# Adapter products with the tokens as stationary operand, beside the main products, in a two-layer LoRA kernel on one core

## The chip, the cores and the metric

The kernel runs on one core of one Trainium2 chip. The time is the device time of one execution in microseconds; lower is better. Matrix products run on TensorE (PE in the profile). In front of each matmul its stationary operand (up to 128 rows by 128 columns) is loaded into the array by a weight load, which the profile lists as an engine of its own, PEld. The moving operand (up to 512 columns) is then streamed through. VectorE (DVE) and ScalarE (ACT) do elementwise work, GpSimd (POOL) and SyncE (SP) mostly issue DMAs here.

## The reference

Two linear layers with a residual each, each with a low-rank adapter that is picked per batch entry:

```python
# x: (8, 256, 1024), one adapter index per batch entry and layer, rank 16
x = x + (x @ W.T + b) + 2 * (x @ A0[i0]) @ B0[i0]          # layer 0
x = x + (x @ W1.T + b1) + (x @ A1[i1].T) @ B1[i1].T        # layer 1
```

## The kernel before

The two layers are folded into one. A first part (up to about 130 us) multiplies the two matrices (I + W0) and (I + W1) into one 1024 by 1024 matrix D, and makes for each batch the low-rank remainder of both adapters: per batch entry 16 columns from layer 0 and 16 columns g that carry layer 1's adapter back through layer 0, with 98 rows (`STACK` = 6 x 16 + 2) on the other side, `rb`, that hold the ranks' second factors and the bias in split form. Every float32 operand is split into a high and a low part of type float32r (`hi`, `lo`), and a product is hi x hi + hi x lo + lo x hi.

The second part runs over the 8 batches `b` of 256 tokens. The main product (256 x 1024 by 1024 x 1024) is done as Strassen-Winograd: seven products `p1` to `p7` of half size. Each (`product`, L855 to L863) is 12 matmuls with 512 moving columns: four blocks k of the contraction, three passes each, on L860 (hi x hi), L861 (hi x lo), L862 (lo x hi). The tokens are stationary (128 token columns of `xa` or of a sum S1 to S4), the weights move. The quarters of the input are A11, A21, A12, A22, where the first digit is the half of the tokens `q`.

The adapters' first factors are multiplied by `h_product` (L869 to L881): there the factors `aa` are stationary and the tokens move, 16 matmuls with 256 moving columns on L880, into bank 6 or 7. DVE then splits the 32 rows of the sum (`stack_h`, L583 to L596) into `h_stack`, and four matmuls per batch on L867 (`ranks`) add the low-rank part and the bias into the four output quarters. The bias part that passes through layer 1's adapter is added to the bias rows in the first part: L847 multiplies `t_blk` by `b1_raw` in plain float32, beside L846.

Order and waiting are written by hand: each engine has its own list of instructions, with semaphores between them. Per batch from the second on PE does p1, h_product, p6, p2 and its rank, p5, p7, p4 and its rank, `fill_z` (a rank), p3 and its rank. SP issues in each batch, after the store of the batch before, the four loads of the next batch's quarters in the order A11, A21, A12, A22 (`load_x`, L209 to L217). DVE's list for a batch interleaves the low parts (`low_x`, L534), the sums S1 to S4 (L541 to L558), `factors` of the next batch (L573 to L577) and the output combinations (`make_u2`, `make_u4`, `make_u3`, `put_c21`, `put_c22`, `put_c12`, L606 to L635). ACT makes the high parts (`high_x`, L376), `keep_p1` and `put_c11`.

Of the kernel before, what the change touches and what calls it, by code (L numbers as in the profile page):

```python
# [23 lines left out]
def lora_pair(nc, xT, W0, W1T, A0, B0T, A1T, B1, b0, b1, idx0, idx1, out):  # L24
# [12 lines left out]
    AA_W = KT * 4 * RK + 4 * RK  # L37
# [6 lines left out]
    with ExitStack() as ctx:  # L44
# [11 lines left out]
        xa = sb("xa", [P, 2, 4, QW], F32R)  # L56
        a1 = sb("a1", [P, KT, 2 * BR], F32R)
        b0w = sb("b0w", [P, KT, 2 * BR + 2], F32R)
        aa = sb("aa", [P, 2, AA_W], F32R)
# [8 lines left out]
        h_sum = sb("h_sum", [2 * RK, T], F32)  # L68
        t_blk = sb("t_blk", [P, B], F32)
# [12 lines left out]
        h_tmp = scratch[0:32, 0:T]  # L82
# [23 lines left out]

        def x_op(j, part):
            if j <= A22:
                return xa[:, part, j, :]
            at = (3 * KH + j - S1) * HALF  # L110
            return w1[:, part, at:at + HALF]
# [17 lines left out]
        X, Z, Y, V, W = (banks[i] for i in (2, 3, 4, 5, 0))  # L129
# [42 lines left out]
        ones_set = sem("ones_set")  # L172
        pad_set = sem("pad_set")
        aa_hi = sem("aa_hi")
        aa_ready = sem("aa_ready")
        op_hi = [sem(f"op_hi{j}") for j in range(8)]
        op_lo = [sem(f"op_lo{j}") for j in range(8)]
        s_made = {j: sem(f"s_made{j}") for j in (S1, S2, S3, S4)}
        h_summed = sem("h_summed")
        h_moved = sem("h_moved")  # L180
        h_added = sem("h_added")
        h_hi = sem("h_hi")
        h_ready = sem("h_ready")
        p_done = [sem(f"p_done{n}") for n in range(8)]
        z_full = sem("z_full")
# [21 lines left out]
        def _(sp):  # L207
            def load_x(b):
                for j in (A11, A21, A12, A22):  # L209
                    if b >= 1:  # L210

                        sp.wait_ge(op_lo[j], b)
                        for s in {A11: (S2, S3), A21: (S1, S3), A12: (S4,), A22: (S1,)}[j]:
                            sp.wait_ge(s_made[s], b)
                        if j in (A21, A12):
                            sp.wait_ge(op_lo[S3 if j == A21 else S4], b)
                    sp.dma_start(xr[:, j, :], xT[b, :, j, :]).then_inc(x_landed[j], DMA)  # L217

            def load_rb(b):
                if b >= 2:  # L220
                    sp.wait_ge(p_done[3], b - 1)
                    sp.wait_ge(p_done[4], b - 1)
                    sp.wait_ge(p_done[2], b - 1)
                    sp.wait_ge(z_full, b - 1)
# [94 lines left out]
        def _(act):  # L319
# [43 lines left out]
            def high_x(j, b):  # L363
# [4 lines left out]
                if b >= 1:  # L368

                    if j == A21:  # L370
                        act.wait_ge(h_summed, b)
                    else:
                        act.wait_ge(p_done[LAST_USE[j]], b)
                    if j <= A22:
                        act.wait_ge(h_summed, b)
# [14 lines left out]
            def put_c11(b):  # L390
                act.wait_ge(p_done[2], b + 1)
# [3 lines left out]

            for k in range(KT):
# [17 lines left out]
            for j in (A11, A21, A12, A22):  # L414
                high_x(j, 0)

# [23 lines left out]
            high_t(T3)  # L440
            put_c11(0)
            for j in (A11, A21, A12, A22, S2, S1):
                high_x(j, 1)
            for b in range(1, B):
                if b == 1:
                    for j in (S4, S3):
                        high_x(j, 1)
                else:
                    high_x(S4, b)
                keep_p1(b)  # L450
                if b + 1 < B:
                    high_x(A11, b + 1)
                    high_x(A21, b + 1)
                    high_x(S2, b + 1)
                put_c11(b)
                if b + 1 < B:
                    high_x(A12, b + 1)
                    high_x(S1, b + 1)
                    high_x(S3, b + 1)
                    high_x(A22, b + 1)  # L460

        @block.vector
        def _(dve):
# [86 lines left out]
            def sum_s3(b):  # L550

                dve.wait_ge(op_lo[A21], b + 1)
# [12 lines left out]
            def factors(b):  # L565
                s = b % 2
                to = aa[:, s, 0:KT * 4 * RK].rearrange("p (k c) -> p k c", k=KT)
                g = g_all[:, :, b * RK:(b + 1) * RK]
                a0 = a0_raw[:, s, :].rearrange("p (k r) -> p k r", k=KT)
                dve.wait_ge(a0_landed[s], (b // 2 + 1) * DMA)  # L570
                if b >= 2:
                    dve.wait_ge(h_summed, b - 1)
                nc.vector.tensor_copy(to[:, :, 0:RK], a0).then_inc(aa_hi, 1)  # L573
                nc.vector.tensor_copy(to[:, :, RK:2 * RK], g).then_inc(aa_hi, 1)
                dve.wait_ge(aa_hi, b * 2 + 2)
                nc.vector.tensor_tensor(to[:, :, 3 * RK:4 * RK], g, to[:, :, RK:2 * RK], ALU.subtract)
                nc.vector.tensor_tensor(to[:, :, 2 * RK:3 * RK], a0, to[:, :, 0:RK], ALU.subtract).then_inc(aa_ready, 1)  # L577

            def stack_h(b):
                s = b % 2  # L580
                bank = banks[6 + s]
                dve.wait_ge(h_summed, b + 1)
                nc.vector.tensor_copy(h_tmp, bank[2 * RK:4 * RK, 0:T]).then_inc(h_moved, 1)  # L583
                dve.wait_ge(h_moved, b + 1)
                nc.vector.tensor_tensor(h_sum[:, :], bank[0:2 * RK, 0:T], h_tmp, ALU.add).then_inc(h_added, 1)
                dve.wait_ge(h_added, b + 1)
                if b >= 2:

                    dve.wait_ge(p_done[2], b - 1)
                    dve.wait_ge(p_done[3], b - 1)  # L590
                    dve.wait_ge(p_done[4], b - 1)
                    dve.wait_ge(z_full, b - 1)
                nc.vector.tensor_copy(h_stack[s][0:2 * RK, :], h_sum[:, :]).then_inc(h_hi, 1)
                nc.vector.tensor_copy(h_stack[s][2 * RK:4 * RK, :], h_sum[:, :]).then_inc(h_hi, 1)
# [413 lines left out]
```

## Time and profile before

| | |
|---|---|
| median of 3 runs | 313.38 us (311.9 to 313.47) |
| the profiled execution, device time | 312.38 us |
| its span, first to last instruction | 310.8 us |
| PE busy | 298.8 us, 96% of the span |
| DVE busy | 193.7 us, 62% |
| ACT busy | 89.7 us, 29% |

The span is the time between the first and the last instruction of that one execution; the device time holds 1.6 us more. Times of instructions below count from the span's start. A matmul's listed duration covers its way through the array, which overlaps the next matmul's; what a matmul costs in a row of matmuls is the distance from its start to the next one's start.

### The profile page before, as it was taken

Reading aid. Unit: us, or ns where it says so; the run is one execution under the profiler, and the core shown is the slowest. Engines: PE = TensorE matmul, PEld = TensorE weight load, DVE = VectorE, ACT = ScalarE, POOL = GpSimd, SP = SyncE. Lnnn points to the kernel's source line nnn. Section 1 sums busy time; section 2 is a strip of 40 time slices with the busy share of each in tenths; the row PEclk is TensorE's granted clock in tenths of the full one; section 3 lists DMA queues with packets and bytes.
Section 4 is the critical chain, followed back from the end, with each engine's and each line's share of the span. In section 5 each row is a group of like instructions: output and inputs, shape, how many; then the busy total and the mean of one; then the engine's idle time right before and its main releaser. Section 6 shows DMA issues by size and latency. Waiting matters only on the chain.

```text
span 310.8 us, 3985 instructions
## 1 busy us (share of the span) xinstructions
PE 298.8 (96%) x1420; PEld 247.6 (80%) x1420; DVE 193.7 (62%) x325; ACT 89.7 (29%) x142; POOL 18.5 (6%) x43
## 2 busy tenths in 40 slices
PE   0999999999999999998999999999999999999995
PEld 0888898888887488886888888888888888888884
DVE  4777624994749362188896776487486485585312
ACT  4555424112123302293224123232232322232000
POOL 2443140000000010000000000000000000000000
PEclk9999999999999999999999999999999999999999
DMA  7996140000000155504054360440641621602002
GB/s 268 382 347 226 48 159 12 0 0 2 0 0 3 17 178 209 166 0 135 0 194 138 115 184 34 152 147 34 187 141 38 211 78 70 219 35 85 18 34 101
DMA packets 14456, 33.94 MB, mean 109 GB/s; under 512 B 2117, under 2 KB 2117, under 8 KB 14438
## 3 DMA queue, kind: packets, MB, share of 16 engines
q1 hardware_dynamic: 13414, 31.60, 30.1%
q0 software_dynamic: 1024, 2.10, 2.1%
q8 instruction: 11, 0.18, 0.2%
q14 instruction: 7, 0.06, 0.1%
HBM read 22.09 MB, written 11.60 MB: 108 GB/s over the span
## 4 chain that ended last, share of the span: by engine, by line
PE 92%; DVE 4%; ACT 2%; DMA 1%; issue 0%; SPq 0%
PE bank L766 29%; PE bank L861 16%; PE bank L860 16%; PE bank L862 16%; PE bank L880 4%; PE bank L778 3%; PE bank L867 3%; DMA stage<-W1T 1%; PE bank L835 1%; PE bank L837 1%; PE bank L836 1%; PE bank L780 1%; DVE w L562 1%; PE bank L808 1%; PE bank L846 1%; PE bank L847 1%
## 5 line engine op out<-in xcount | busy, mean ns | idle before, releaser
L766 PE MATMUL bank<-w,w_hi 128*128 128x512 f32 x256 | 80.7, 397 | 7.0 <-ACT w L325 7.0
L766 PEld LDWEIGHTS bank<-w,w_hi 128*128 128x128 f32 x256 | 48.7, 192 | 17.9 <-ACT w L325 7.0
L766 PE MATMUL bank<-w,w_lo 128*128 128x512 f32 x128 | 50.1, 391 | 0.0
L376 ACT CAST xa<-xr 128x512 fp32r<-128x512 f32 x32 | 19.6, 621 | 33.9 <-PE bank L867 15.0
L766 PEld LDWEIGHTS bank<-w,w_lo 128*128 128x128 f32 x128 | 24.2, 189 | 5.1
L861 PE MATMUL bank<-w_lo,w 128*128 128x512 f32 x64 | 25.1, 392 | 0.0
L862 PE MATMUL bank<-w_hi,w 128*128 128x512 f32 x64 | 25.0, 391 | 0.0
L860 PE MATMUL bank<-w_hi,w 128*128 128x512 f32 x64 | 25.0, 391 | 0.0
L861 PE MATMUL bank<-w 128*128 128x512 f32 x64 | 25.0, 391 | 0.0
L860 PE MATMUL bank<-w 128*128 128x512 f32 x64 | 25.0, 391 | 0.0
L860 PE MATMUL bank<-w_hi,xa 128*128 128x512 f32 x64 | 25.0, 390 | 0.0
L861 PE MATMUL bank<-w_lo,xa 128*128 128x512 f32 x64 | 24.9, 390 | 0.0
L862 PE MATMUL bank<-w 128*128 128x512 f32 x64 | 24.9, 389 | 0.0
L862 PE MATMUL bank<-w_hi,xa 128*128 128x512 f32 x64 | 24.9, 389 | 0.0
L534 DVE TENSOR_TENSOR xa<-xr,xa 128x512 fp32r<-128x512 f32 x32 | 21.1, 685 | 1.4 <-ACT xa L376 1.4
L529 DVE SCALAR_TENSOR_TENSOR rows<-w,b_raw,rows 128x1024 f32<-128x1024 f32 x16 | 20.5, 1283 | 0.4
L376 ACT CAST w<-rows 128x512 fp32r<-128x512 f32 x16 | 9.8, 621 | 37.7 <-DVE rows L548 25.9
L534 DVE TENSOR_TENSOR w<-rows,w 128x512 fp32r<-128x512 f32 x16 | 11.0, 687 | 11.9 <-ACT w L376 11.9
L376 ACT CAST w<-xr 128x512 fp32r<-128x512 f32 x16 | 9.8, 621 | 29.5 <-PE bank L867 15.8
L880 PEld LDWEIGHTS bank<-xa,aa 128*128 128x128 f32 x128 | 16.2, 189 | 0.6
L880 PE MATMUL bank<-xa,aa 128*128 128x256 f32 x128 | 16.4, 281 | 0.0
L778 PE MATMUL bank<-a,w_hi 128*128 128x256 f32 x64 | 15.5, 327 | 0.0
(119 smaller groups left out, 487.0 us busy)
## 6 DMA issues: line engine op xcount, KB each, us to landing
xr<-xT SPq DMA_DIRECT2D x32, 256.0 KB, 4.4
out<-stage SPq DMA_DIRECT2D x28, 256.0 KB, 2.1
stage<-W SPq DMA_DIRECT2D x8, 512.0 KB, 4.9
stage<-W1T SPq DMA_DIRECT2D x8, 512.0 KB, 6.0
a<-rb_rows SPq DMA_DIRECT2D x8, 392.0 KB
rb_rows<-a SPq DMA_DIRECT2D x3, 512.0 KB
rb_rows<-b0w SPq DMA_DIRECT2D x3, 512.0 KB
out<-rows SPq DMA_DIRECT2D x4, 256.0 KB, 2.2
```

Of the source, the lines that this page charges most:

```text
L376: nc.scalar.copy(x_op(j, 0), raw(j)).then_inc(op_hi[j], 1)
L529: nc.vector.scalar_tensor_tensor(out=bias_sum, in0=part[:, k, :], scalar=b0_raw[:, k:k + 1], in1=bias_sum, op0=ALU.mult, op1=ALU.add).then ...
L534: nc.vector.tensor_tensor(x_op(j, 1), raw(j), x_op(j, 0), ALU.subtract).then_inc(op_lo[j], 1)
L562: nc.vector.tensor_tensor(t_whole(t, 1), t_raw[t][:, :, :].rearrange("p k n -> p (k n)"), t_whole(t, 0), ALU.subtract).then_inc(t_lo, 1)
L766: return mm(d_bank(m, h)[:, :], left[:, m, k * P:(k + 1) * P], right[:, k, h * HALF:(h + 1) * HALF], start=start, stop=stop)
L778: last = mm(bank[:, 0:2 * BR], w0_hi[:, m, cols], a1[:, k, :], start=(k == 0), stop=(k == KT - 1))
L780: mm(bank[:, 0:BR], w0_lo[:, m, cols], a1[:, k, 0:BR], start=False, stop=False)
L860: mm(bank[:, :], hi, t_op(t, 0, k), start=(start and k == 0), stop=False, skip_group_check=not start)
L861: mm(bank[:, :], hi, t_op(t, 1, k), start=False, stop=False, skip_group_check=not start)
L862: last = mm(bank[:, :], lo, t_op(t, 0, k), start=False, stop=(k == KH - 1), skip_group_check=not start)
L867: return mm(bank[:, :], h_stack[b % 2][0:STACK, q * P:(q + 1) * P], rb[b % 2][:, h * HALF:(h + 1) * HALF], start=False, stop=True, skip_gr ...
L880: last = mm(banks[6 + s][:, 0:T], aa[:, s, k * 4 * RK:k * 4 * RK + P], xa[:, part, 2 * kh:2 * kh + 2, tok], start=(k == 0 and part == 0), ...
```

## The change

The first factors' product changes sides. For each 128-token column block that `p1`, `p2`, `p4` and `p5` load anyway, two more matmuls stand between the three of the product: the token block's high part by 64 columns of `aa` (`h_high`: 32 factor columns' high parts and 32 low parts), and its low part by the 32 high columns (`h_low`). The result has tokens on its rows: bank 6 for the first half of the tokens (`q` 0, closed in p2), bank 7 for the second (`q` 1, from S1 in p5 and A22 in p4, for which `factors` makes a third set of factor columns, the difference of the two halves). Quarter A21 is then needed in no operand, and its high and low parts go. `split_h` on DVE splits each half (128 rows by 32 columns, five operations), `turn_h` transposes it by a matmul against an identity in float32r (98 columns stationary, 128 moving), `stack_h` on ACT copies it into `h_stack`. The ranks' matmuls are taken out of p2, p3 and p4 and moved later.

The bias term through layer 1's adapter, L847's two float32 matmuls, goes; in its place `t_sum` is split, turned by one matmul with an identity (a row ahead of the `r` products), copied by ACT to `t_rows`, and added to the sum by a matmul of two stationary rows and 16 moving columns, once per half (`ones_row`, `t_rows`).

On PE, where a batch begins. Before: the end of the batch before (L867), p1, the adapter product (L880), then p6:

```order
L867 MATMUL bank<-a,b0w 128x512
L860 MATMUL bank<-w_hi,xa 128x512 [waits op_lo0,made_c11]
L861 MATMUL bank<-w_lo,xa 128x512
L862 MATMUL bank<-w_hi,xa 128x512
...
L880 MATMUL bank<-xa,aa 128x256 [waits op_lo2,op_lo3,op_lo1,h_added,op_lo0,aa_ready]
L880 MATMUL bank<-xa,aa 128x256 x15
L860 MATMUL bank<-w 128x512 [waits op_lo5,kept_u3]
```

The adapter product stands there as one block of 16.

After, the same place: L896, L901 and L906 are the three passes of a product, L913 is `h_high`, L916 `h_low`, L909 the bias rows:

```order
L927 MATMUL bank<-a,b0w 128x512 [waits h_stacked,kept_u4]
L896 MATMUL bank<-w_hi,xa 128x512 [waits h_read0,op_lo0,made_c11,aa_ready]
L913 MATMUL bank<-aa,xa 128x64
L901 MATMUL bank<-w_lo,xa 128x512
L916 MATMUL bank<-aa,xa 128x32
L906 MATMUL bank<-w_hi,xa 128x512
L909 MATMUL bank<-t_rows,ones_row 128x16
L896 MATMUL bank<-w_hi,xa 128x512
L913 MATMUL bank<-aa,xa 128x64
```

Sixteen matmuls in one block have become 34 small ones per batch, each between two matmuls of 512 columns.

On PE behind the last auxiliary product of the first part (L806), after the change; the row with 2x128 is new, and the next row stood directly behind L806's before:

```order
L857 MATMUL bank<-ident_r,t_parts 2x128 [waits aux_done,consts_set,t_split]
L865 MATMUL bank<-rows,s_t 128x512 [waits b1_landed,st_step,t4_made]
```

The small turn of `t_parts` waits for `aux_done` 8, the end of DVE's `g_add(7)`, which L865 does not wait for.

On DVE in batch 0, after the change; L637 is `make_u2`, L644 `make_u4`, L666 `put_c12`, L569 and L576 the sums S1 and S2 of batch 1, L562 the low parts of A11, S2, A12, and L617 to L627 `split_h(0, 1)`:

```order
L637 TENSOR_TENSOR stage<-bank,rows 128x512 [waits t_lo,kept_p1,p_done6]
L644 TENSOR_TENSOR stage<-bank,stage 128x512 [waits kept_u2,p_done5]
L666 TENSOR_TENSOR stage<-bank,stage 128x512 [waits kept_u4,full_c12]
L569 TENSOR_TENSOR rows<-xr 128x512 [waits op_lo4,x_landed3,x_landed1]
L576 TENSOR_TENSOR rows<-rows,xr 128x512 [waits s_made4,op_lo5,x_landed0]
L562 TENSOR_TENSOR xa<-xr,xa 128x512 [waits op_hi0]
L562 TENSOR_TENSOR w<-rows,w 128x512 [waits op_hi5]
L562 TENSOR_TENSOR xa<-xr,xa 128x512 [waits op_hi2]
L617 COPY h_small<-bank 128x32 [waits h_summed1]
L619 TENSOR_TENSOR h_sum<-bank,h_small 128x32 [waits h_moved1]
L624 CAST h_parts<-h_sum 128x32 [waits h_read1]
```

The second split of batch 0 stands behind eight operations of 512 columns. In the later batches the sums S1 and S2 of the next batch have moved ahead of `make_u2` and of the first split.

The diff, cut to its core:

```diff
             def factors(b):
...
+                nc.vector.tensor_tensor(f_raw[:, KT:both, :], f_raw[:, KH:KT, :], f_raw[:, 0:KH, :], ALU.subtract
+                                        ).then_inc(f_step, 1)
...
+            def split_h(b, q):
+
+                dve.wait_ge(h_summed[q], b + 1)
+                nc.vector.tensor_copy(h_small[:, q, :], H[q][:, FW:2 * FW]).then_inc(h_moved[q], 1)
+                dve.wait_ge(h_moved[q], b + 1)
+                nc.vector.tensor_tensor(h_sum[:, q, :], H[q][:, 0:FW], h_small[:, q, :], ALU.add
+                                        ).then_inc(h_read[q], 1)
...
+            pe.wait_ge(t_split, 2)
+            pe.wait_ge(consts_set, 3)
+            pe.wait_ge(aux_done, 8)
+            mm(banks[7][0:2, 0:P], t_parts[:, :], ident_r[:, :], start=True, stop=True).then_inc(t_turned, 1)
...
-                mm(bank[0:B, :], ones_b[:, :], bias_sum[:, cols], start=True, stop=False)
-                mm(bank[0:B, :], t_blk[:, :], b1_raw[:, cols], start=False, stop=True).then_inc(c_summed, 1)
+                mm(bank[0:B, :], ones_b[:, :], bias_sum[:, cols], start=True, stop=True).then_inc(c_summed, 1)
...
                     mm(bank[:, :], hi, t_op(t, 0, k), start=(start and k == 0), stop=False, skip_group_check=skip)
+                    if closes:
+                        h_low(b, h, k, lo)
+                    elif h is not None:
+                        h_high(b, h, k, hi, opens, False)
+                    mm(bank[:, :], hi, t_op(t, 1, k), start=False, stop=False, skip_group_check=skip)
+                    if closes:
+                        h_high(b, h, k, hi, False, True).then_inc(h_summed[h[0]], 1)
+                    elif h is not None:
+                        h_low(b, h, k, lo)
+                    last = mm(bank[:, :], lo, t_op(t, 0, k), start=False, stop=(k == KH - 1), skip_group_check=skip)
+                    if opens:
+
+                        mm(H[h[0]][:, RK:FW], ones_row[:, :], t_rows[:, b * RK:(b + 1) * RK], start=False, stop=False)
...
+            def h_high(b, h, k, hi, start, stop):
+                return mm(H[h[0]][:, 0:2 * FW], hi, aa[:, b % 2, h[1] * KH + k, :], start=start, stop=stop)
+
+            def h_low(b, h, k, lo):
+                return mm(H[h[0]][:, 0:FW], lo, aa[:, b % 2, h[1] * KH + k, 0:FW], start=False, stop=False)
+
+            def turn_h(b, q):
+                pe.wait_ge(h_split[q], b + 1)
+                if 2 * b + q > 0:
+                    pe.wait_ge(h_stacked, 2 * b + q)
+                mm(H_TURNED[0:STACK, q * P:(q + 1) * P], h_parts[:, q, :], ident_r[:, :], start=True, stop=True
+                   ).then_inc(h_turned, 1)
...
-            def h_product(b):
...
-                for k in range(KT):
...
             for b in range(1, B):
                 p1(b)
-                h_product(b)
                 p6(b)
                 p2(b)
                 p5(b)
+                turn_h(b, 0)
+                p4(b)
+                rank11(b)
                 p7(b)
-                p4(b)
-                fill_z(b)
-                p3(b)
+                turn_h(b, 1)
+                p3(b, first)
+                rank21(b)
+                rank22(b)
+                p3(b, second)
+                rank12(b)
```

## Rows read from the trace of the kernel before

**Rows 1.** The page: busy shares, and the chain that ended last, by engine.

```profile
PE 298.8 (96%) x1420; PEld 247.6 (80%) x1420; DVE 193.7 (62%) x325; ACT 89.7 (29%) x142; POOL 18.5 (6%) x43
...
PE 92%; DVE 4%; ACT 2%; DMA 1%; issue 0%; SPq 0%
```

**Rows 2.** TensorE's clock in 40 slices, in tenths of full speed, from the page.

```profile
PEclk9999999999999999999999999999999999999999
```

**Rows 3.** Timeline of PE in one batch: start us, us, line, operands, count.

```profile
175.54 0.40 PE L860 MATMUL bank<-w_hi,xa 128*128 128x512 f32 x1
...
178.28 2.05 PE L880 MATMUL bank<-xa,aa 128*128 128x256 f32 x16
180.17 0.40 PE L860 MATMUL bank<-w 128*128 128x512 f32 x1
...
197.51 0.40 PE L860 MATMUL bank<-w_hi,xa 128*128 128x512 f32 x1
```

**Rows 4.** Timeline of PE, an auxiliary product of the first part between 512-column matmuls.

```profile
75.07 0.39 PE L766 MATMUL bank<-w,w_lo 128*128 128x512 f32 x1
75.30 0.28 PE L778 MATMUL bank<-a,w_hi 128*128 128x256 f32 x1
75.41 0.22 PE L780 MATMUL bank<-a,w_lo 128*128 128x128 f32 x1
...
77.14 0.63 PE L766 MATMUL bank<-w,w_hi 128*128 128x512 f32 x2
```

**Rows 5.** Timeline of the weight loads (PEld) at the same place.

```profile
75.08 0.19 PEld L778 LDWEIGHTS bank<-a,w_hi 128*128 128x128 f32 x1
75.30 0.19 PEld L780 LDWEIGHTS bank<-a,w_lo 128*128 128x128 f32 x1
75.42 0.19 PEld L778 LDWEIGHTS bank<-a,w_hi 128*128 128x128 f32 x1
```

**Rows 6.** Timeline of PE and PEld inside a product.

```profile
158.17 0.40 PE L860 MATMUL bank<-w 128*128 128x512 f32 x1
158.17 0.19 PEld L861 LDWEIGHTS bank<-w 128*128 128x128 f32 x1
```

**Rows 7.** Timeline of PE at the bias rows.

```profile
105.55 1.02 PE L847 MATMUL bank<-rows,t_blk 128*8 128x512 f32 x2
106.41 1.02 PE L846 MATMUL bank<-rows,ones_b 128*8 128x512 f32 x2
```

**Rows 8.** Timelines of PE and DVE behind the last auxiliary product.

```profile
91.73 1.02 PE L832 MATMUL bank<-rows,s_t 128*128 128x512 f32 x2
...
92.35 0.28 DVE L492 TENSOR_TENSOR g_all<-bank,scratch 128x128 f32<-128x128 f32 x1
```

**Rows 9.** Timeline of PE in batch 0, and where batch 1 begins.

```profile
130.11 0.39 PE L860 MATMUL bank<-w_hi,xa 128*128 128x512 f32 x1
...
141.54 0.50 PE L867 MATMUL bank<-a,b0w 98*128 98x512 f32 x1 [1.19 <-DVE b0w L596]
...
153.56 0.39 PE L860 MATMUL bank<-w_hi,xa 128*128 128x512 f32 x1
```

**Rows 10.** Timeline of DVE in batch 0.

```profile
136.58 2.29 DVE L562 TENSOR_TENSOR w<-stage,w 128x2048 fp32r<-128x2048 f32 x1
...
142.13 4.49 DVE L562 TENSOR_TENSOR w<-stage,w 128x2048 fp32r<-128x2048 f32 x2
```

**Rows 11.** Groups of DVE by line: busy us, mean ns of one, idle before.

```profile
L583 DVE COPY scratch<-bank 32x256 f32<-32x256 f32 x8 | 3.3, 416 | 19.4 <-PE bank L880 19.3
...
L606 DVE TENSOR_TENSOR stage<-bank,rows 128x512 f32<-128x512 f32 x4 | 2.7, 686 | 1.2 <-PE bank L862 1.2
```

**Rows 12.** Timeline of SP at the next batch's loads.

```profile
177.03 1.83 SPq L217 DMA_DIRECT2D xr<-xT  x4
```

**Rows 13.** The loads' time from issue to landing, from the line's own view.

```profile
DMA to landing us min/median/max: 3.1/4.4/5.8
```

**Rows 14.** Timeline of DVE at the end.

```profile
307.58 0.69 DVE L635 TENSOR_TENSOR stage<-bank,stage 128x512 f32<-128x512 f32 x1 [1.74 <-PE bank L867]
```

More of the change, by code:

```diff
@@ L105, in t_whole @@
             return w1[:, part, at:at + KH * HALF]
+        XA = (A11, A12, A22)
         def x_op(j, part):
-            if j <= A22:
-                return xa[:, part, j, :]
+            if j in XA:
+                return xa[:, part, XA.index(j), :]
             at = (3 * KH + j - S1) * HALF
@@ L390, in put_c11 @@
             def put_c11(b):
[L391 removed]
+                act.wait_ge(full["c11"], b + 1)
                 if b >= 2:
@@ L413, in _ @@
             aux_copy(8)
-            for j in (A11, A21, A12, A22):
+            for j in XA:
                 high_x(j, 0)
+            act.wait_ge(t_turned, 1)
+            nc.scalar.copy(t_rows[:, :], banks[7][0:2, 0:P]).then_inc(t_rows_made, 1)
             for h in range(NH):
@@ L676, in _ @@
             bias_add(7)
-            for j in (A11, A21, A12, A22):
+            for j in XA:
                 low_x(j, 0)
@@ L708, in _ @@
             low_t(0, T2)
[L710 to L713 removed]
+            split_h(0, 0)
             low_x(S3, 0)
@@ L718, in _ @@
             make_u4(0)
-            for j in (A11, A21, A12, A22):
-                low_x(j, 1)
+            put_c12(0)
             sum_s1(1)
             sum_s2(1)
-            make_u3(0)
-            low_x(S2, 1)
-            put_c21(0)
-            put_c22(0)
-            put_c12(0)
+            for j in (A11, S2, A12):
+                low_x(j, 1)
+            split_h(0, 1)
             sum_s3(1)
@@ L756, in _ @@
                 put_c22(b)
-                if b + 1 < B:
-                    low_x(A22, b + 1)
                 put_c12(b)
@@ L909, in p3, with rank12 @@
                     pe.wait_ge(made["c12"], b)
-                product(b, S4, B22, W, True)
-                ranks(b, 0, 1, W).then_inc(p_done[3], 1)
+                last = product(b, S4, B22, W, True, ks)
+                if ks[-1] == KH - 1:
+                    last.then_inc(p_done[3], 1)
+            def rank12(b):
+                ranks(b, 0, 1, W).then_inc(full["c12"], 1)
             def p4(b):
@@ L917, in p4, with rank21 @@
                     pe.wait_ge(made["c21"], b)
-                product(b, A22, T4, V, True)
-                ranks(b, 1, 0, V).then_inc(p_done[4], 1)
+                product(b, A22, T4, V, True, h=(1, 2)).then_inc(p_done[4], 1)
+            def rank21(b):
+                ranks(b, 1, 0, V).then_inc(full["c21"], 1)
             def p5(b):
@@ L942, in p7 @@
                 pe.wait_ge(kept["u2"], b + 1)
-                product(b, S3, T3, Y, False).then_inc(p_done[7], 1)
-            pe.wait_ge(pad_set, 2)
+                last = product(b, S3, T3, Y, False, ks)
+                if ks[-1] == KH - 1:
+                    last.then_inc(p_done[7], 1)
+            first, second = range(KH // 2), range(KH // 2, KH)
             p1(0)
-            h_product(0)
             p5(0)
@@ L950, in _ @@
             p3(0)
+            turn_h(0, 0)
             p6(0)
+            rank11(0)
+            rank12(0)
             p4(0)
-            fill_z(0)
-            p7(0)
+            p7(0, first)
+            turn_h(0, 1)
+            p7(0, second)
+            rank21(0)
+            rank22(0)
             for b in range(1, B):
                 p1(b)
-                h_product(b)
                 p6(b)
```

238 lines of the change are left out of this document (122 added, 116 removed).

## The prediction

> **What bounds the kernel now.** I read the busy shares and the chain that ended last first: PE is busy 96% of the span and carries 92% of that chain [rows 1], and its granted clock stays at the full level, 2.4 GHz, in all slices [rows 2]. So the time is the sum of what PE issues, plus the few places where it waits. Next the timeline of one batch: p1 begins at 175.54 and the next batch's p1 at 197.51, 21.97 us, in which PE never stops. p1 takes 178.28 - 175.54 = 2.74 us, 0.228 us for each of 12 matmuls with 512 columns, and the adapter product 180.17 - 178.28 = 1.89 us, 0.118 us for each of 16 with 256 columns [rows 3]. DVE at 62% has room. The question is what a matmul with 64 or 32 moving columns costs between two of 512.
>
> **What a small matmul costs.** The trace has none that small, but it has 256 and 128 columns in turn. A stretch of 16, half of them 256 and half 128 wide, begins at 75.30 and the next 512-column matmul at 77.14: 1.84 us, 0.115 us each [rows 4]. Their columns are 3072, at 2.4 GHz 1.28 us, so columns do not set that pace. The weight loads do: those of consecutive matmuls start 0.12 us apart (75.30, 75.42) [rows 5], one per matmul, also for L860 and L861, which have the same tokens stationary (PE and PEld both count 1420) [rows 1, 6]. And a load does not run further ahead than one matmul: L780's load starts at 75.30, the moment L778 begins, although the load before it started at 75.08 [rows 4, 5]; in a product L861's load starts with L860's matmul at 158.17 [rows 6]. Under a 512-column matmul (0.228 us) a load of 0.116 us is hidden. Under a matmul of 64 or 32 columns it is not: the next product matmul's load can start only when the small one starts, and takes its 0.116 us. So each small matmul adds 0.116 us, whatever its width. The bounds: from below its columns alone, with the 0.013 us by which 0.228 us exceeds 512 columns at 2.4 GHz rounded up to 0.015: 0.042 us for 64 columns, 0.028 for 32, 0.022 for 16, 0.068 for 128. From above 0.12 us, the spacing of the loads as printed, unless the small form is treated in another way (a rival). I take 0.116, since the 128-column rows are nearest and are already bound by the load.
>
> The Trainium skill states another floor: by its page "TensorE: Matmul & The Clock Gate", section "Wait — 56ns, not 53.3ns?", matmuls start as little as 25 ns apart however small they are, and N columns cost N/2.4 + 2.5 ns. By that a batch's 36 new matmuls cost 1.0 us, less than the 1.89 us that go, and the kernel gets some 7 us faster; the rows with 128 columns (0.115 us where this rule has 0.056) speak against it, since each matmul here has its own load.
>
> **The change part by part.**
> 1. *The adapter product.* Removed per batch: 1.89 us [rows 3]. Added per batch: 16 pairs of h_high and h_low, 2 bias rows, 2 turns, 36 matmuls at 0.116 = 4.18 us. Net +2.29 us per batch, 8 batches: **+18.3 us**, all on PE's path. The low bound by columns is 16 x 0.042 + 16 x 0.028 + 2 x 0.022 + 2 x 0.068 = 1.30 us per batch, net -0.59, in all -4.7 us.
> 2. *The bias rows.* L847's two float32 matmuls cost 106.41 - 105.55 = 0.86 us each (the row's x2 is one instruction in two records) [rows 7]: **-1.7 us**. The added turn of t_parts costs 0.12 us.
> 3. *The wait in front of that turn.* It waits for `aux_done` 8. PE reaches this place at 91.73; the g_add that ends this count runs from 92.35 to 92.63 on DVE, behind low_bottom(6) [rows 8]. Everything behind it in PE's list, the r products first, waits too: 0.9 us, **+0.9 us**. The matmuls of r never waited for it before. Bounds 0.8 and 1.1.
> 4. *Batch 0, the wait that goes.* The rank in p2 waited for `stack_h`: PE idle 1.19 us, and the batch took 153.56 - 130.11 = 23.45 us, 1.48 more than a steady one [rows 9]. In the new order the first split has p3 to hide in: **-1.5 us**.
> 5. *Batch 0, the wait that comes.* With T0 the start of p1: p1 and p5 take 2.74 + 9 x 0.116 = 3.8 each, p2 2.74 + 0.93 = 3.7, so the first sum is whole at T0 + 11.2. DVE is free by then (its 2048-column L562 ended at 138.87, T0 + 8.8) [rows 10]. A split is five operations: 256 columns take 0.416 us and 512 take 0.686 [rows 11], so 0.00105 us a column over 0.15 us fixed, 0.18 for 32, and 0.03 between dependent ones: 1.05 us, T0 + 12.2. Then low_x(S3) 0.6, two L562 4.5 [rows 10], T0 + 17.3; then the eight operations of 512 columns at 0.69 to 0.72, of which two wait for ACT's part, T0 + 23.0; then the split, T0 + 24.1. PE: p1, p5, p2 11.2, p3 2.74, turn 0.12, p6 2.74, two ranks 0.47, p4 3.67, half of p7 1.37: it reaches `turn_h(0, 1)` at T0 + 22.3. It waits 1.8 us: **+1.8 us**; queued behind it are the second half of p7, the two ranks and batch 1. Bounds 0.8 (operations back to back at 0.60) and 3 (a load that lands late holds sum_s1).
> 6. *Later batches.* DVE now does the next batch's S1 and S2 ahead of the first split; S1 needs A22. SP issues the four loads 1.5 us to 3.3 us behind p1's start, the last one's issue beginning near +2.9 [rows 3, 12], and landing takes 4.4 to 5.8 us [rows 13]: A22 is there by +7.3 to +8.7. Then S1, S2, A11, make_u2, S2's low part, 5 x 0.65 = 3.2, and the split 1.05: done by +11.6 to +13.0. PE reaches `turn_h(b, 0)` at 3.8 + 2.74 + 3.7 + 3.7 = +13.9. It fits, with 0.9 to 2.3 us to spare. `turn_h(b, 1)` has p7 and a rank (3.0 us) for a split of 1.05. So these cost nothing; if the cover goes they cost the lateness of A22 itself. In batch 1 the loads start late, since DVE left batch 0 late: **+0.4 us**, bounds 0 and 1.5.
> 7. *DVE and ACT.* A21's low and high parts go (0.69 and 0.62 us a batch); the splits' ten small operations come to 2.1 us against 2.0 before, the copies of `stack_h` to ACT. Both stay off the path. The end keeps its order: the last rank, `put_c12` [rows 14], its store, and the two stores before it are done sooner or at the same time: 0.
>
> **The sum.** 18.3 - 1.7 + 0.1 + 0.9 - 1.5 + 1.8 + 0.4 = +18.3 us. Against the profiled execution's 312.38 us: 330.7 us. That execution lies 1.0 us under the median of the runs shown, so the median may be up to 1 us more; I take 331.
>
> **The rivals.**
> - *The loads are hidden (faster).* If the load of the small matmul and the one behind it both fit under the 512-column matmul in front, or a load of tokens that are already in place is left out, a small matmul costs its columns. The point from which it decides is a price under 0.05 us per small matmul. For it: three matmuls in five of a block share their stationary tokens. Against it: the loads' start with the matmul before, and L860 and L861, each with a load of its own [rows 4 to 6]. It gives 312.4 - 4.7 + 0.0 (terms 2 to 6) = 308 us. Chance 0.08.
> - *Half hidden.* A price of 0.08 us per small matmul, halfway between the bounds, gives 36 x 0.08 = 2.9 us per batch, +1.0 net: 320.3 us. Chance 0.05. The skill's same page, section "Back-to-back issue gap", has about 81 ns for pairs of load and matmul at 128 columns, which is this case; the rows show 115.
> - *A turn waits in every batch.* If A22 lands 1 us or more behind +8.7, or a split takes 2 us instead of 1, `turn_h(b, 0)` holds PE 1 to 2 us in seven batches: 338 to 345 us. For it: DVE's list is in strict order and S1 now stands first. Chance 0.06.
> - *The small float32r form is slow.* If 64 or fewer columns went as plain float32 does, in four passes of columns and loads as on L846, a small matmul would cost near 0.4 us and the kernel over 400 us. The 128-column rows show nothing of that. Chance 0.01.
> - That the change does not do what it says: the new order shows each matmul where the diff puts it.
>
> **How the numbers follow.** The forecast's own case has 0.80: 331 us. Its own range, with 0.113 to 0.12 us per small matmul (288 of them, -0.9 to +1.2), the waits (-1.8 to +3) and 1 us between executions, is 327 to 336. I take 325 to 336, a little to the half-hidden case; the rest is outside. A measurement of this kernel can tell about 0.5% from no change. Faster by over 0.5% is the first rival, 0.08; slower by over 0.5% is all the others, 0.91; within 0.5% 0.01.
>
> **What would show it.** In the changed kernel's trace: L913, L916 and L909 rows each followed 0.11 to 0.12 us later by the next matmul, with one load each; PE and PEld both at about 1577 (1420 - 128 - 4 + 288 + 1); a batch of 24.2 to 24.3 us; PE idle about 0.9 us in front of L857 and 1 to 3 us in front of the second L922 of batch 0, both put down to DVE; no idle time at L922 later. A batch under 22 us would show the first rival, idle time on each first L922 of a batch the third. Wrong is the forecast if loads run two matmuls ahead.

## The result and the profile after

The changed kernel takes 337.48 us in the median of 5 runs (335.97 to 341.43) against 312.74 for the kernel before: ratio 1.078, 95% interval 1.076 to 1.080. It is slower, as forecast, by 24.7 us instead of 18.3, and 1.5 us above the range. The profiled execution took 341.43 us (span 339.7); it has a stretch in which PE ran at half its clock, which not every execution has, so the sizes of steady batches below are read outside that stretch.

The page's lines on PE and on its clock, the ones of [rows 1, 2]:

```profile
PE 324.6 (96%) x1577; PEld 268.3 (79%) x1577; DVE 191.3 (56%) x364; ACT 88.3 (26%) x152; POOL 18.6 (5%) x43
...
PEclk9999999999999999999978999999999999999999
```

PE is still the bound, with 157 more matmuls and as many more loads; two slices of the clock are below 9.

The timeline of PE and PEld where a steady batch begins (start us, us, line, operands), to be held against [rows 3 to 6]:

```profile
187.24 0.39 PE L896 MATMUL bank<-w_hi,xa 128*128 128x512 f32 x1
...
187.47 0.19 PE L913 MATMUL bank<-aa,xa 128*128 128x64 f32 x1
187.47 0.19 PEld L901 LDWEIGHTS bank<-w_lo,xa 128*128 128x128 f32 x1
187.50 0.47 PE L901 MATMUL bank<-w_lo,xa 128*128 128x512 f32 x1
...
187.81 0.18 PE L916 MATMUL bank<-aa,xa 128*128 128x32 f32 x1
187.81 0.19 PEld L906 LDWEIGHTS bank<-w_hi,xa 128*128 128x128 f32 x1
187.84 0.48 PE L906 MATMUL bank<-w_hi,xa 128*128 128x512 f32 x1
188.24 0.18 PEld L909 LDWEIGHTS bank<-t_rows,ones_row 2*128 2x128 f32 x1 [0.24 <-issue]
188.24 0.27 PE L909 MATMUL bank<-t_rows,ones_row 2*128 2x16 f32 x1
188.44 0.19 PEld L896 LDWEIGHTS bank<-w_hi,xa 128*128 128x128 f32 x1
188.44 0.50 PE L896 MATMUL bank<-w_hi,xa 128*128 128x512 f32 x1
...
189.12 0.19 PEld L906 LDWEIGHTS bank<-w_hi,xa 128*128 128x128 f32 x1
189.23 0.19 PEld L896 LDWEIGHTS bank<-w_hi,xa 128*128 128x128 f32 x1
189.46 0.39 PE L896 MATMUL bank<-w_hi,xa 128*128 128x512 f32 x1
...
190.37 0.39 PE L896 MATMUL bank<-w_hi,xa 128*128 128x512 f32 x1
```

How to read it: the load of the matmul behind a small one starts when the small one starts (L901's at 187.47), as the rows before had it. L901's listed start of 187.50 lies 0.03 us behind that, and its duration is 0.47 instead of 0.39; I read the 0.08 us more as its wait for its load. A block without bias rows takes 190.37 - 189.46 = 0.91 us: three times 0.227 and two small ones at 0.115. The first block takes 189.46 - 187.24 = 2.22 with the second, 1.31 alone: L909 costs 0.40 us. In the block without bias rows the load behind L906's starts 0.11 us behind it (189.12, 189.23). L909's load starts 0.43 us behind L906's (187.81, 188.24), with nothing loading for the last 0.24 us, and the next 128-row load starts another 0.20 us later (188.44).

The batches, counted from 0: first the first turns of batches 4 and 5; then batch 0 with its second turn, and batch 1 with its first turn, each with what held it.

```profile
251.43 0.22 PE L922 MATMUL bank<-ident_r,h_parts 128*98 128x128 f32 x1
...
276.27 0.22 PE L922 MATMUL bank<-ident_r,h_parts 128*98 128x128 f32 x1
```

```profile
130.82 0.39 PE L896 MATMUL bank<-w_hi,xa 128*128 128x512 f32 x1
...
154.90 0.30 PE L922 MATMUL bank<-ident_r,h_parts 128*98 128x128 f32 x1 [1.04 <-DVE h_parts L627]
...
156.95 0.40 PE L896 MATMUL bank<-w_hi,xa 128*128 128x512 f32 x1
...
173.87 0.43 PE L922 MATMUL bank<-ident_r,h_parts 128*98 128x128 f32 x1 [2.20 <-DVE h_parts L627]
```

A steady batch takes 24.84 us (21.97 in [rows 3]). Batch 0 takes 156.95 - 130.82 = 26.13 with 1.04 us idle. Batch 1 takes 187.24 - 156.95 = 30.29, 5.45 more than a steady one: 2.20 listed as idle, and most of the other 3.25 from the clock (in a_pad32 below, whose clock stayed full, batch 1 has 2.11 us idle and takes 183.66 - 156.42 = 27.24 us, 2.40 more than a steady one). SP and DVE in batch 1 show where the 2.20 come from:

```profile
158.77 2.77 SPq L243 DMA_DIRECT2D out<-stage  x3
161.65 1.85 SPq L233 DMA_DIRECT2D xr<-xT  x4
...
169.73 0.69 DVE L569 TENSOR_TENSOR rows<-xr 128x512 f32<-128x512 f32 x1 [7.31 <-DMA xr<-xT]
```

The four loads start 4.7 us behind p1 instead of 1.5 [rows 3, 12], since the stores of batch 0 stand ahead of them in SP's list; the last is issued by 163.5 and S1 begins at 169.73, 6 us later (the longest landing of L233's loads in this trace is 6.5 us). S1 keeps DVE still for 7.3 us, while the split waits behind it. The clock in stretches (us, busy us and counts of PE, PEld, DVE, ACT, POOL, clock, DMA):

```profile
165.00:170.00 5.00, 5.00 (x29) 4.15 (x27) 0.27 (x1) 0.62 (x1) 0.00 (x0) 1.00 0.77 222
170.00:175.00 5.00, 2.80 (x14) 2.22 (x13) 4.80 (x13) 1.80 (x4) 0.00 (x0) 0.84 0.01 2
175.00:180.00 5.00, 5.00 (x16) 4.13 (x16) 1.82 (x4) 0.12 (x1) 0.00 (x0) 0.50 0.00 0
180.00:187.24 7.24, 7.24 (x33) 5.95 (x33) 4.25 (x10) 1.89 (x4) 0.00 (x0) 0.98 0.12 44
```

The granted clock falls to half (1.2 GHz) in this stretch, in which PE had stood still from 171.67 to 173.87, and is full (2.4 GHz) again soon after 180; in 175 to 180 PE gets 16 matmuls done, where it had done 29 in 165 to 170.

The wait in front of the turn of `t_parts`, from the waits by engine (us in total, times, longest):

```profile
PE bank L857 <- DVE g_all L520: 0.9, 1, 0.9
```

### The profile page after: what moved, and what is told of

The parts are those of the page before. It is cut to its first block, busy times and chain, and to the rows that moved or that the text cites. A ratio compares the mean times of both kernels' runs of the same rounds, so it can differ in the third digit from the quotient of the medians.

```text
span 339.7 us, 4386 instructions
## 1 busy us (share of the span) xinstructions
PE 324.6 (96%) x1577; PEld 268.3 (79%) x1577; DVE 191.3 (56%) x364; ACT 88.3 (26%) x152; POOL 18.6 (5%) x43
## 4 chain that ended last, share of the span: by engine, by line
PE 48%; DMA 2%; DVE 2%; SPq 1%; issue 0%; DVEq 0%
PE bank L906 15%; PE bank L901 15%; PE bank L896 13%; PE bank L927 2%; DMA xr<-xT 2%; PE bank L913 1%; PE bank L909 1%; SPq L243 1%; PE bank L916 0%; PE bank L922 0%; SPq L233 0%; DVE rows L569 0%; DVE stage L661 0%; DVE stage L656 0%; DVE stage L666 0%
## 5 line engine op out<-in xcount | busy, mean ns | idle before, releaser
L906 PE MATMUL bank<-w_hi,xa 128*128 128x512 f32 x64 | 30.5, 476 | 0.0
L901 PE MATMUL bank<-w_lo,xa 128*128 128x512 f32 x64 | 30.5, 476 | 0.0
L794 PEld LDWEIGHTS bank<-w,w_lo 128*128 128x128 f32 x128 | 24.6, 192 | 5.3
L906 PE MATMUL bank<-w_hi,w 128*128 128x512 f32 x64 | 27.9, 436 | 0.0
L901 PE MATMUL bank<-w_lo,w 128*128 128x512 f32 x64 | 27.8, 435 | 0.0
L896 PE MATMUL bank<-w_hi,w 128*128 128x512 f32 x64 | 26.3, 410 | 0.0
L896 PE MATMUL bank<-w_hi,xa 128*128 128x512 f32 x64 | 26.0, 406 | 0.0
L569 DVE TENSOR_TENSOR rows<-xr 128x512 f32<-128x512 f32 x8 | 5.5, 690 | 34.9 <-DMA xr<-xT 34.9
L896 PE MATMUL bank<-w 128*128 128x512 f32 x64 | 25.1, 392 | 0.0
L906 PE MATMUL bank<-w 128*128 128x512 f32 x64 | 25.0, 391 | 0.0
L901 PE MATMUL bank<-w 128*128 128x512 f32 x64 | 25.0, 391 | 0.0
L913 PEld LDWEIGHTS bank<-aa,xa 128*128 128x128 f32 x96 | 18.7, 195 | 2.9
L916 PEld LDWEIGHTS bank<-aa,xa 128*128 128x128 f32 x96 | 18.9, 197 | 0.7
L562 DVE TENSOR_TENSOR xa<-xr,xa 128x512 fp32r<-128x512 f32 x24 | 16.3, 686 | 4.9 <-ACT xa L385 4.9
L913 PE MATMUL bank<-aa,xa 128*128 128x64 f32 x96 | 18.7, 194 | 0.0
L916 PE MATMUL bank<-aa,xa 128*128 128x32 f32 x96 | 17.3, 180 | 0.0
L415 ACT CAST b0w<-bank 98x128 fp32r<-98x128 f32 x16 | 4.3, 266 | 46.5 <-PE bank L922 46.5
```

Of the source, the lines that this page charges most:

```text
L415: nc.scalar.copy(h_stack[b % 2][0:STACK, q * P:(q + 1) * P], H_TURNED[0:STACK, q * P:(q + 1) * P]).then_inc(h_stacked, 1)
L562: nc.vector.tensor_tensor(x_op(j, 1), raw(j), x_op(j, 0), ALU.subtract).then_inc(op_lo[j], 1)
L569: nc.vector.tensor_tensor(s_raw[S1], xr[:, A21, :], xr[:, A22, :], ALU.add).then_inc(s_made[S1], 1)
L794: return mm(d_bank(m, h)[:, :], left[:, m, k * P:(k + 1) * P], right[:, k, h * HALF:(h + 1) * HALF], start=start, stop=stop)
L896: mm(bank[:, :], hi, t_op(t, 0, k), start=(start and k == 0), stop=False, skip_group_check=skip)
L901: mm(bank[:, :], hi, t_op(t, 1, k), start=False, stop=False, skip_group_check=skip)
```

## The experiments

My theory after the two traces: (a) each small matmul costs one load, 0.115 us, whatever its width; (b) the 16 bias-row matmuls cost 0.40 us each, because an operand with two rows is not loaded under the running matmul ahead of it; (c) the waits of batches 0 and 1 come from the order of DVE's list, and the clock follows the second. Rivals: the price is that of mixing widths or of columns, L909 is dear for its 16 columns, and the waits would only move.

**Leaving out the bias rows.** The kernel leaves out the bias term through layer 1's adapter.

```diff
-                    if opens:
-
-                        mm(H[h[0]][:, RK:FW], ones_row[:, :], t_rows[:, b * RK:(b + 1) * RK], start=False, stop=False)
```

> The changed kernel without the 16 bias-row matmuls L909 (two stationary rows, 16 moving columns, two per batch); the bias term through layer 1's adapter is left out of the result. In the changed kernel's trace such a matmul costs 1.31 - 0.91 = 0.40 us where the forecast had 0.116. My theory (L909 is the mis-sized term): 16 x 0.40 = 6.4 us less than the changed kernel, 331 us, and a steady batch of 24.84 - 0.8 = 24.04 us. Rival (L909 costs 0.116 like the other small ones, and the missing time lies elsewhere): 1.9 us less, a batch of 24.6 us.

Measured 331.86 us, ratio 1.060 (1.056 to 1.064), 5.6 us less than the changed kernel. The first turns of two batches:

```profile
244.88 0.22 PE L919 MATMUL bank<-ident_r,h_parts 128*98 128x128 f32 x1
...
269.02 0.22 PE L919 MATMUL bank<-ident_r,h_parts 128*98 128x128 f32 x1
```

A batch takes 24.14 us, 0.70 less: 0.35 us per L909, near the 0.40 read from the rows and far from 0.116. The term was mis-sized as the theory says. This run too has a stretch at half clock, behind 1.55 us idle in batch 1.

**128 rows instead of two.** The 126 added rows of t_rows are set to zero once.

```diff
-        t_rows = sb("t_rows", [2, P], F32R)
-        ones_row = sb("ones_row", [2, P], F32R)
+        t_rows = sb("t_rows", [128, P], F32R)
+        ones_row = sb("ones_row", [128, P], F32R)
...
+            nc.vector.memset(t_rows[:, :].bitcast(F32), 0.0).then_inc(consts_set, 1)
...
```

> The changed kernel with ones_row and t_rows as 128 rows, of which 126 of t_rows are zero, so that L909 has 128 stationary rows instead of two and computes the same. Theory: the short stationary operand (two rows) is what costs, so L909 falls to 0.115 us, a steady batch to 24.27 us and the time by 16 x 0.285 = 4.6 us, to 333 us. Rival: the 16 moving columns or the narrow output cost, or the switch to other tiles; then nothing changes (24.84 us a batch, 337.5 us).

Measured 335.66 us (331.89 to 337.03), ratio 1.069 (1.062 to 1.075). The same place in its timeline, and its first turns:

```profile
184.93 0.39 PE L897 MATMUL bank<-w_hi,xa 128*128 128x512 f32 x1
...
185.51 0.19 PEld L907 LDWEIGHTS bank<-w_hi,xa 128*128 128x128 f32 x1
...
185.62 0.19 PEld L910 LDWEIGHTS bank<-t_rows,ones_row 128*128 128x128 f32 x1
185.85 0.17 PE L910 MATMUL bank<-t_rows,ones_row 128*128 128x16 f32 x1
...
186.87 0.39 PE L897 MATMUL bank<-w_hi,xa 128*128 128x512 f32 x1
...
247.48 0.22 PE L923 MATMUL bank<-ident_r,h_parts 128*98 128x128 f32 x1
...
271.82 0.22 PE L923 MATMUL bank<-ident_r,h_parts 128*98 128x128 f32 x1
```

Two blocks take 186.87 - 184.93 = 1.94, less 0.91: 1.03 for the first, so L910 with the same 16 columns costs 0.12 us, and its load now starts 0.11 us behind L907's (185.51, 185.62) instead of 0.43. A batch takes 24.34 us (24.27 expected). The median gained only 1.8 us of the 4 that 8 batches give. The clock is a likely reason: its profiled run too has a stretch at half clock behind the wait of batch 1 (1.92 us idle there). Its fastest run, 331.89 us, is 4.1 us under the fastest of the changed kernel.

**32 rows instead of two**, the same edit with 32.

> As a_pad128, with 32 rows instead of 128. It tells whether the short operand costs for having less than the full 128 rows, or only when it is very short. Theory A (a load of another number of rows cannot start under the running matmul): L909 stays at 0.40 us, a steady batch 24.84 us, 337.5 us. Theory B (only fewer than 32 rows cost): 0.115 us, a batch of 24.27 us, 332 to 335.7 us like a_pad128.

Measured 337.19 us, ratio 1.080 (1.075 to 1.085). Its L910, from the view of the line (duration ns min/median/max, first and last start), and its first turns:

```profile
L910 PEld LDWEIGHTS bank<-t_rows,ones_row x16: 181/181/181, 131.3 to 319.3; 32*128 32x128 f32 x16
...
247.85 0.22 PE L923 MATMUL bank<-ident_r,h_parts 128*98 128x128 f32 x1
...
272.69 0.22 PE L923 MATMUL bank<-ident_r,h_parts 128*98 128x128 f32 x1
```

24.84 us a batch: 32 rows cost what two cost. The load itself is no longer than others (0.18 us listed, 0.19 for 128 rows); what differs is when it starts: here too nothing loads for 0.24 us in front of L910, while in a_pad128 no idle time stands there. By the Trainium skill, page "TensorE: Matmul & The Clock Gate", section "LDWEIGHTS (loading the stationary operand)", a load of 32 by 128 takes as long as one of 128 by 128; the listed durations agree with that, and the price of the matmul, three times as high, does not follow from it. The ranks' operand with 98 rows does not pay it (0.23 to 0.24 us behind a product, L927 in the timelines as L867 before). Somewhere between 32 and 98 rows lies the border; where was not tried.

**Wide small matmuls.** What they sum is then not the adapters' product.

```diff
-                return mm(H[h[0]][:, 0:2 * FW], hi, aa[:, b % 2, h[1] * KH + k, :], start=start, stop=stop)
+                return mm(H[h[0]][:, 0:8 * FW], hi, aa[:, b % 2, h[1] * KH:(h[1] + 1) * KH, :], start=start, stop=stop)
```

and h_low in the same way.

> The changed kernel with 256 moving columns in every h_high and h_low instead of 64 and 32; what they sum is then not the adapters' product. Theory (the load sets the price): 256 columns take 0.118 us in the kernel before, so at most 256 x 0.003 = 0.8 us more than the changed kernel, 338 us. Rival (the price is columns plus something fixed): 0.080 us more for each h_high and 0.093 for each h_low, 128 of each, +22 us, 360 us.

Measured 339.36 us, ratio 1.086 (1.083 to 1.089). One block in its timeline:

```profile
185.25 0.39 PE L896 MATMUL bank<-w_hi,xa 128*128 128x512 f32 x1
185.48 0.28 PE L913 MATMUL bank<-aa,xa 128*128 128x256 f32 x1
185.60 0.39 PE L901 MATMUL bank<-w_lo,xa 128*128 128x512 f32 x1
...
186.18 0.40 PE L896 MATMUL bank<-w_hi,xa 128*128 128x512 f32 x1
```

0.93 us a block against 0.91: four and eight times the columns cost 0.01 us each. A batch takes 25.21 us by two of its turns (248.09 and 273.30), 0.37 more; over 8 batches 3.0 us: more than the 0.8 expected, and nowhere near the 22 of a price by columns. The median grew by 1.9 us only; PE idles 0.97 and 1.49 us in batches 0 and 1 here, 0.8 less in all than in the changed kernel. So a narrower moving operand saves almost nothing below 256 columns.

**No h_low.** The 128 matmuls of the tokens' low part are left out.

```diff
-                    if closes:
-                        h_low(b, h, k, lo)
-                    elif h is not None:
+                    if h is not None and not closes:
                         h_high(b, h, k, hi, opens, False)
...
-                    elif h is not None:
-                        h_low(b, h, k, lo)
```

> The changed kernel without the 128 h_low matmuls (the tokens' low part times the factors is left out). Theory (one load each, 0.115 us): 128 x 0.115 = 14.7 us less, 322.8 us, a steady batch of 23.0 us; the stall of batch 1 may shrink or grow by a microsecond. Rival (a small matmul costs its columns, 0.028 us, and the rest is a cost of mixing that h_high alone brings): 3.6 us less, 334 us.

Measured 325.28 us, ratio 1.041 (1.035 to 1.046). A batch takes 23.00 us by its first turns (287.41 and 310.41), 1.84 less, 0.115 for each h_low, as expected. The time lies 2.5 us above the expected one. The waits grew, batch 0's from 1.04 to 1.52 us and batch 1's from 2.20 to 3.12:

```profile
170.76 0.30 PE L918 MATMUL bank<-ident_r,h_parts 128*98 128x128 f32 x1 [3.12 <-DVE h_parts L627]
```

A faster PE reaches the turn earlier, while the load hardly moves (S1 begins 12.2 us behind batch 1's p1, 12.8 before): a part of what PE saves there is given back as idle time. Behind the 3.12 us the granted clock fell again (0.66 in 170 to 175), which costs this execution 1.7 us more in batch 1 (24.69 us between the first turns of batches 1 and 2, against 23.00).

**The order of DVE's list in batches 0 and 1.**

```diff
-            for j in (A11, S2, A12):
-                low_x(j, 1)
-            split_h(0, 1)
+            low_x(A11, 1)
+            split_h(0, 1)
+            low_x(S2, 1)
+            low_x(A12, 1)
...
                     factors(b + 1)
+                if b == 1:
+                    make_u2(b)
+                    split_h(b, 0)
+                if b + 1 < B:
                     sum_s1(b + 1)
...
```

> The changed kernel with DVE's list reordered in batches 0 and 1 alone: the second split of batch 0 stands directly behind A11's low part, and in batch 1 make_u2 and the first split stand ahead of the sums S1 and S2 that wait for a load. Theory (the order of DVE's list makes the two waits of PE, 1.04 us and 2.2 us, and the half-clock stretch behind the second one follows from it): no idle time at either L922, PE's clock full in all slices, 3.2 us less without and up to 3.3 us more with the clock, 331 to 334 us. Rival (the wait moves: S1, now later, holds p6 or the first split of batch 2, and DVE stays behind): PE idles as long one batch later, 336 to 338 us.

Measured 334.06 us (333.66 to 334.82), ratio 1.067 (1.066 to 1.069), with the full clock in all slices of its page. DVE in batch 1:

```profile
166.15 0.19 DVE L617 COPY h_small<-bank 128x32 f32<-128x32 f32 x1 [2.67 <-PE bank L920]
...
167.22 0.69 DVE L569 TENSOR_TENSOR rows<-xr 128x512 f32<-128x512 f32 x1 [0.22 <-DMA xr<-xT]
```

The split is done before A22 lands, S1 waits 0.22 us, and PE is idle at no L922. 3.4 us are gone by the medians, at the upper end of the time expected (331 to 334); 3.2 are the two listed waits, and batches 0 and 1 take 24.85 and 24.88 us.

**The same edit in batch 1 alone.**

> a_order's edit in batch 1 alone; the second split of batch 0 stands where the change has it. Theory (the two waits are separate, batch 1's comes from S1's wait for the load of A22): the 1.04 us idle in batch 0 stays, none in batch 1, full clock: a_order plus 1.0 us, 335.1 us. Rival (batch 1's wait is the lateness that batch 0 hands on): idle time shows up in batch 1 again, at another instruction, 336 to 337.5 us.

Measured 335.42 us, ratio 1.074 (1.072 to 1.075). PE idles once, 1.04 us in front of batch 0's second turn, as in the changed kernel, and not in batch 1; the clock line of its page has a 9 in all slices. So the two waits are separate, and the fall of the clock goes with the second.

**The turn of t_parts behind the r products.**

```diff
-            pe.wait_ge(aux_done, 8)
-            mm(banks[7][0:2, 0:P], t_parts[:, :], ident_r[:, :], start=True, stop=True).then_inc(t_turned, 1)
-
             pe.wait_ge(t4_made, 2)
...
+            pe.wait_ge(aux_done, 8)
+            mm(banks[7][0:2, 0:P], t_parts[:, :], ident_r[:, :], start=True, stop=True).then_inc(t_turned, 1)
             pe.wait_ge(d_lo[B11], 3)
```

ACT's copy of its result moves behind the copies of r and b1 in the same way.

> The changed kernel with the small turn L857 and its wait for aux_done moved behind the r products, and ACT's copy of it behind the copies of r and b1. Theory: the wait of 0.9 us in front of it vanishes, since g_add has long ended there, and nothing else waits: 0.9 us less, 336.6 us. Rival (what stands behind is bound by DVE and ACT anyway, or the copy in ACT's list now delays the bias rows): no change.

Measured 335.9 us, ratio 1.074 (1.071 to 1.076). The median is 1.6 us under the changed kernel's, the fastest runs of both 0.7 us apart (335.29, 335.97). No wait in front of this matmul is left in the list of waits. The times cannot weigh the 0.9 us by itself: this execution also idles 1.32 us in batch 1 instead of 2.20, with the clock full, and p1 of batch 0 starts at 129.15 here, but anywhere from 129.38 to 130.90 in six executions that have the same first part as the changed kernel (its own among them). The 0.9 us is consistent, not measured.

**All three repairs.**

> The changed kernel with all three repairs: 128 stationary rows for the bias rows, the DVE order of a_order, the late turn. It computes the same. Theory: 4.6 + 3.2 + 0.9 us less and no half-clock stretch, 337.5 - 8.7 = 328.8 down to 326 us, a steady batch of 24.27 us; it stays slower than the kernel before by the weight loads, 8 x 2.29 = 18.3 us less the 1.7 + 1.5 us saved. Rival (something else of the new order costs): over 331 us.

Measured 328.42 us, ratio 1.051 (1.049 to 1.054). First turns of two batches:

```profile
264.04 0.22 PE L930 MATMUL bank<-ident_r,h_parts 128*98 128x128 f32 x1
...
288.35 0.22 PE L930 MATMUL bank<-ident_r,h_parts 128*98 128x128 f32 x1
```

24.31 us a batch. Against the kernel before (312.89 us beside it): 8 x (24.31 - 21.97) = 18.7, less 1.7 + 1.5 for the bias rows and batch 0's old wait, plus 0.1 for the turn, is +15.6; measured +15.5. What is left is the price of the small matmuls.

**The kernel before, with batch 0's rank behind p3.**

```diff
                 product(b, A12, B21, X, False)
+                if b > 0:
+                    rank11(b)
+
+            def rank11(b):
                 pe.wait_ge(h_ready, b + 1)
...
                 product(b, S4, B22, W, True)
+                if b == 0:
+                    rank11(b)
```

> The kernel before with one edit: in batch 0 the rank of p2 is issued behind p3's product instead of ahead of it, so that p3 hides stack_h. Theory (the 1.19 us of idle time there were all that held PE, as term 4 of the prediction has it): 1.2 to 1.5 us less, 311.4 us. Rival (DVE's list is the bound up to p4 and p7 of batch 0, and the wait moves there): no change.

Measured 311.39 us, ratio 0.9949 (0.9933 to 0.9965). PE over batch 0 in its windows view:

```profile
130.00:160.00 30.00, 30.00 (x149) 25.36 (x148) 26.44 (x39) 14.88 (x20) 0.00 (x0) 1.00 0.29 94
```

30 us busy of 30: the wait is gone and did not move.

**And with the bias term as a column that DVE adds.**

```diff
-                mm(bank[0:B, :], t_blk[:, :], b1_raw[:, cols], start=False, stop=True).then_inc(c_summed, 1)
...
+            mm(banks[7][0:2 * RK, 0:B], pick[:, :], t_blk[:, :], start=True, stop=True).then_inc(t_picked, 1)
...
-                nc.vector.tensor_tensor(h_sum[:, :], bank[0:2 * RK, 0:T], h_tmp, ALU.add).then_inc(h_added, 1)
+                nc.vector.scalar_tensor_tensor(out=h_sum[:, :], in0=bank[0:2 * RK, 0:T], scalar=t_cols[:, b:b + 1],
+                                               in1=h_tmp, op0=ALU.add, op1=ALU.add).then_inc(h_added, 1)
...
```

`pick` is a constant that DVE makes, and ACT copies the new matmul's result to `t_cols`.

> The kernel before with the deferred rank of batch 0 and with the bias term through layer 1's adapter moved out of the bias rows as in the change, but at no price per batch: one float32 matmul turns it into a column per batch, and DVE's sum of the adapter product (L585) adds that column as its scalar. It computes the same. Theory: L847's two matmuls (1.7 us) go for one of 8 columns (0.2 to 0.5 us) and nothing else on PE: 1.2 to 1.5 us less than b_defer's 311.39, about 310.0 us, 2.9 us less than the kernel before. Rival (the new copy on ACT ahead of the bias rows, or the sum with a scalar, holds something): no less than b_defer, 311.4 us.

Measured 309.68 us, ratio 0.9910 (0.9894 to 0.9926): 2.9 us under the kernel before (312.58 beside it), the fastest of all. In its timeline the new matmul stands where two of 0.86 us stood [rows 7]:

```profile
104.41 0.23 PE L855 MATMUL bank<-t_blk,pick 128*32 128x8 f32 x2
104.49 1.88 PE L862 MATMUL bank<-rows,ones_b 128*8 128x512 f32 x4
106.30 0.73 PE L779 MATMUL bank<-w,w_hi 128*128 128x512 f32 x2
```

## Why the prediction came out as it did

1. *What a small matmul costs.* Right. 0.116 was taken, 0.115 measured, from the timeline, from h_low left out and from widths that hardly matter. The rule by which a small matmul costs its columns with a floor of 25 ns (the Trainium skill, "TensorE: Matmul & The Clock Gate", "Wait — 56ns, not 53.3ns?") does not hold for matmuls that each have their own load: L916's 32 columns cost 0.115 us. That it is the load that costs, and not another fixed price of the same size, is read from the rows (a load starts when the small matmul in front of it starts); no run changes the load alone. The working's 0.013 us, by which 0.228 us exceeds 512 columns at 2.4 GHz, is 0.015 (0.228 less 0.213); the bounds used 0.015.
2. *The adapter product, +18.3.* The step that failed. The sum priced "2 bias rows" with the 34 others at 0.116 us and set 0.12 as the upper bound. They have two stationary rows; the nearest rows it had, L780's with 128 columns, have 128 stationary rows, and it took the width of the moving operand for all that differs. Measured 0.40 us each, 24.84 us a batch instead of 24.26: 8 x 0.58 = 4.6 us missing. a_pad128 shows the cause: with 128 rows and the same 16 columns the price is 0.12. By this term alone the forecast would have been 335.6, still inside the range; batch 1's wait (7 below) takes it out.
3. *The bias rows' two matmuls, -1.7.* Right within what can be told: b_both, with the same removal and a new matmul of about 0.1 us, gains 1.7 us on b_defer by the medians and 1.2 by the ratios of their own calls.
4. *The wait for `aux_done`, +0.9.* Right as the wait is listed, 0.9 us; the times of a_turn_late do not weigh it by themselves.
5. *Batch 0's old wait, -1.5.* Right; b_defer alone gained 1.5 us.
6. *Batch 0's new wait, +1.8.* 1.04 us listed, inside its bounds; the batch takes 1.29 more than a steady one. DVE in batch 0 (T0 = 130.82):

```profile
142.45 0.19 DVE L617 COPY h_small<-bank 128x32 f32<-128x32 f32 x1 [2.90 <-PE bank L913]
...
148.39 0.69 DVE L637 TENSOR_TENSOR stage<-bank,rows 128x512 f32<-128x512 f32 x1
...
154.00 0.18 DVE L617 COPY h_small<-bank 128x32 f32<-128x32 f32 x1
...
154.65 0.19 DVE L627 TENSOR_TENSOR h_parts<-h_sum,h_parts 128x32 fp32r<-128x32 f32 x1
```

   The eight operations took 154.00 - 148.39 = 5.6 us, as the working had it, and the split is done at T0 + 24.0, forecast T0 + 24.1. That is two things that cancel: the two dear L909 put the first sum about 0.5 us later, and a split takes about 0.8 us instead of 1.05, twice. PE reached the turn some 0.6 us later than forecast, by the same two L909.
7. *Batch 1, +0.4, at most 1.5.* The second term that failed: 2.20 us idle, some 2.5 us on the batch at full clock, and about 3 us more in the profiled execution, by the clock. The cause was named (the loads start late because DVE leaves batch 0 late), but its size was not worked out: the loads' start came 3.2 us later than in a steady batch, the last landing took over 6 us, above the 5.8 of [rows 13], and S1 begins at +12.8 instead of +8.7 at the latest, where there were 0.9 us to spare. a_order and a_order1 show the cause: with the split ahead of S1 no idle time is left. That PE's clock could fall behind such a wait was not in any term or bound.
8. *Later batches, 0.* Right: no first or second turn from batch 2 on has idle time in front of it.

Together, the batches by their lengths: 22.96 (8 x 2.87) - 0.7 (the bias rows' two matmuls, the turn of `t_parts` and the wait in front of it) - 1.5 + 1.3 (batch 0) + 2.5 (batch 1) = +24.6 us at full clock, measured +24.7. The agreement to a tenth is partly luck: executions of one kernel differ by more. The rival with waits in every batch did not come true; the rival with hidden loads is excluded by a_wide256 and a_no_low. The rival of a dear small form put all of them near 0.4 us, by four passes, at a chance of 0.01; one in eighteen has that price, and for another reason, since with 128 rows it costs 0.12.

## What to carry to other kernels

Where every matmul brings its own load, count loads before columns: a block of 16 matmuls of 256 columns (1.89 us) was replaced by 34 narrow ones (3.9 us at best), and by a_wide256 the width of the moving operand has almost no part in that price. Price each operand shape by itself: a matmul with few stationary rows between full ones can cost three times what its neighbours do, and padding the operands to 128 rows, with zeros in one of them, took that away here. In an engine with a strict list, an operation that waits for a load should not stand ahead of one that PE waits for.

## What the runs showed that I had not expected

- A matmul with 2 or 32 stationary rows between matmuls with 128 costs 0.35 to 0.40 us, one with 128 rows and the same 16 columns 0.12 us. Nothing loads for 0.24 us in front of its load each time, and the next load starts 0.20 us behind it instead of 0.11. Whether 64 or 96 rows pay it is open; 98 do not.
- PE's granted clock fell to half behind idle stretches of 3.12 (a_no_low), 2.20 (the changed kernel), 1.92 (a_pad128) and 1.55 us (a_no_bias) in batch 1, and stayed full behind 2.11 (a_pad32), 1.49 (a_wide256) and 1.32 us (a_turn_late); it never fell in the five runs of a_order, without such a stretch. What decides is open.
